# Filler products behind the last chunks of an edge pass, and one bank of sums fewer

## The chip, the cores and the metric

The kernel runs on one core of one Trainium2 chip. The metric is the device time of one execution in microseconds (us); lower is better. TensorE is the matrix engine, VectorE, ScalarE and GpSimd are the other three compute engines, SyncE issues transfers.

## What is computed

A graph network of four layers over 3125 nodes of 128 features and 50000 edges, sorted by target node. Each layer normalises the node features, passes them along the edges, sums at the targets and adds the result to the features. The change is in the third layer of the four (the reference's `_L2_gnn_ref`, "layer 2" in the kernel), which has two edge passes. The first one computes, cut to what matters:

```python
def _gat_layer(x, src, dst, W, a_src, a_dst, concat):      # 8 heads
    for h in range(W.shape[0]):
        Wh = x @ W[h]
        e = leaky_relu((Wh @ a_src[h])[src] + (Wh @ a_dst[h])[dst], 0.2)
        att = _seg_softmax(e, dst, n)
        out = segment_sum(att[:, None] * Wh[src], dst, num_segments=n)
...
def _rel_gcn_layer(x, src, dst, w, W):
    deg = segment_sum(w, dst, num_segments=n)
    norm = w / maximum(deg[dst], 1e-16)
    return relu(segment_sum(norm[:, None] * (x @ W)[src], dst, num_segments=n))
...
for i in range(2):
    x1 = _gat_layer(x1, src, dst, *gat_params[i], concat=i != 1)
    x2 = _rel_gcn_layer(x2, src, dst, edge_weight, gcn_params[i])
```

## The kernel before

The edges are cut into NC = 392 chunks of 128, and 8 chunks (BC) make a batch, so 49 batches (NBATCH). An edge pass of layer 2 is the stage `layer2_edges(i, ...)`, with i = 0 for the first and i = 1 for the second. Between the two stands a stage on the nodes (`layer2_nodes0`), behind the second one more and then the diffusion layer. The first pass begins when the tables of the node features lie in memory.

In a pass GpSimd gathers the 128 source rows of each chunk by an indirect transfer (recorded at L229) into a ring of RING = 40 chunks; a chunk's slot is free when TensorE has summed the chunk that stood in it. For each batch VectorE, ScalarE and TensorE work out the attention weights by turns: the windows are transposed on TensorE (L1704) and copied by ScalarE (L1800), the target's part of the logits is looked up (L1711), the logits are formed on VectorE (L1580, needs the gathered rows of the batch), transposed (L1717), scanned for their maxima, neighbouring batches exchange the maxima at their border (L1727 to L1732), and the exponentials are transposed back (L1739).

Then each chunk is summed on TensorE (`sums`). In the first pass VectorE has scaled the gathered rows by the weights (L1626), and TensorE multiplies them with a one-hot matrix of 17 columns: L1753 for the attention part, L1754 for the other, both float32, and L1759 in bf16 for the sums of the weights, which also tells the rest that the chunk is done. In the second pass the scaling is in the one-hot matrix, so that L1756 has 136 columns and L1757 has 17, and L1759 is the same. A float32 product stands in the trace as two records.

The sums of three chunks (PER = 3) stand in one bank of PSUM; with five banks (NBK, bank_of, L1481) the first chunk of a group may begin when ScalarE has stored the last chunk of the group five before. ScalarE stores a chunk (`store`, L1844 and L1847) seven chunks behind TensorE's order, and joins neighbouring groups by keeping the shared column (L1832, L1833), which VectorE adds (L1649, L1650).

The order is written out by hand and is the same on all engines: steps p (one for each batch, and four more) with ten slots q. A slot of TensorE's list may hold the sums of one chunk, then a transpose, look-up or exchange. A batch is looked up in step p = b and its chunks are summed a little over three steps later, so in step 48, the last one with a look-up, TensorE has 34 chunks left.

`busy(...)` (L1691) is a product that nothing reads: identity times a constant piece of memory, written to bank 7 (L1695). Before the change it works in the second pass alone: 24 of 512 columns ahead of the pass, three in each of the first slots, and behind each chunk one of 512, in the first steps also one of 256:

```python
sums(c)
busy(512, *(() if i and p >= min(nodes.begins) else (256,)))
```

Of the kernel before, what the change touches and what calls it, by code (L numbers as in the profile page):

```python
# [19 lines left out]
NC = 392  # L20
WIN = 16
H = 8
BC = 8
# [108 lines left out]
def build(nc, a, out):  # L132
    ctx = ExitStack()
    with ctx:
# [3 lines left out]
        banks = ctx.enter_context(nc.psum_tensor("banks", [P, 8, 512], F32))  # L138
# [39 lines left out]
        identb = keep.get([P], BF16)  # L178
# [1258 lines left out]
        SLOTS, AFTER, LEAD, PER = 10, 11, 2, 3  # L1437

        def layer2_edges(i, begin, nodes):
# [6 lines left out]
            RING = RB * BC  # L1446
# [31 lines left out]
            NGR = -(-NC // PER)  # L1478
            last_of = lambda g: min(PER * g + PER, NC) - 1

            NBK = 4 if i else 5  # L1481
            bank_of = lambda c: (4, 5, 6, 1, 7)[c // PER % NBK]
            sums_in = lambda c: banks[:, bank_of(c), 0:PS].rearrange("p (h w) -> p h w", w=HS)[:, :, c % PER * WIN:c % PER * WIN + WIN + 1]
            weights_in = lambda c: banks[0:3 * (H + 1), bank_of(c), PS + c % PER * WIN:PS + c % PER * WIN + WIN + 1]
            nb0, nc0, ng0, sh0 = i * NBATCH, i * NC, i * NGR, i * (NGR - 1)
# [19 lines left out]
            def g_landed(e, b):  # L1505
                e.wait_ge(of_rows[b % RB], rows0[b % RB] + 16 * BC * (b // RB + 1))
# [177 lines left out]
            def pe(e):  # L1684
                begin(e)
                if i:

                    e.wait_ge(t_made, 1)
                spare = wide.bitcast(BF16)[:, 0:512]

                def busy(*columns):  # L1691

                    if i:
                        for n in columns:
                            e.matmul(banks[:, 7, 0:n], identb, spare[:, 0:n], start=True, stop=True, skip_group_check=True)  # L1695

                busy(*[512] * 24)

                def turn(b):
                    e.wait_ge(e2_windows, nb0 + b + 1)  # L1700
                    if b:
                        e.wait_ge(e2_ot, nb0 + b)
                        e.wait_ge(e2_sum, nb0 + b)
                    e.transpose(banks[:, 0, :].bitcast(BF16)[:, 0:P], OHW[b % 2], identb).then_inc(e2_turned, 1)  # L1704

                def look_up(b):
                    e.wait_ge(e2_ot, nb0 + b + 1)
                    e.wait_ge(e2_bd, nb0 + b + 1)
                    if b:
                        e.wait_ge(e2_sum, nb0 + b)  # L1710
                    e.matmul(banks[:, 0, P:P + BC * H], OT[b % 2], BD[b % 2].rearrange("p j h -> p (j h)"), start=True, stop=True).then_inc(e2_edm, 1)  # L1711

                def turn_logits(b):
                    e.wait_ge(e2_z, nb0 + b + 1)
                    if b:
                        e.wait_ge(e2_ztc, nb0 + b)
                    e.transpose(banks[0:64, 2, 0:P], Z[b % 2], ident).then_inc(e2_zt, 1)  # L1717

                def exchange(b):
                    me = ML[b % R4]  # L1720
                    pr = ML[(b - 1) % R4] if b else None
                    ne = ML[(b + 1) % R4] if b < NBATCH - 1 else None
                    o = banks[0:64, 3, 0:2]
                    e.wait_ge(e2_bw, nb0 + min(b + 2, NBATCH))
                    if b:
                        e.wait_ge(e2_m2, nb0 + b)
                    e.matmul(o[:, 0:1], wide[0:64, P - H:P - H + 64], me[:, P - 1:P], start=True, stop=pr is None)  # L1727
                    if pr is not None:
                        e.matmul(o[:, 0:1], wide[0:64, P + 64 - H:P + 128 - H], pr[:, P - 1:P], start=False, stop=True)
                    x = e.matmul(o[:, 1:2], wide[0:64, P + H:P + H + 64], me[:, 0:1], start=True, stop=ne is None)  # L1730
                    if ne is not None:
                        x = e.matmul(o[:, 1:2], wide[0:64, P - 64 + H:P + H], ne[:, 0:1], start=False, stop=True)  # L1732
                    x.then_inc(e2_ex, 1)

                def turn_back(b):
                    e.wait_ge(e2_exp, nb0 + b + 1)
                    if b:
                        e.wait_ge(e2_a, nb0 + b)
                    e.transpose(banks[:, 3, P:P + 64], DF[b % 2], ident[0:64, 0:64]).then_inc(e2_back, 1)  # L1739

                def sums(c):
                    b, j = divmod(c, BC)
                    k4, k3, g = b % R4, b % R3, c // PER
                    begins = c % PER == 0
                    pv = sums_in(c)
                    rows = G[:, c % RING, :]
                    e.wait_ge(e2_spread, nc0 + c + 1)
                    g_landed(e, b)
                    if begins and g >= NBK:
                        e.wait_ge(e2_sacc, nc0 + PER * (g - NBK + 1))  # L1750
                    if i == 0:
                        e.wait_ge(e2_hi, b + 1)
                        e.matmul(pv[:, 0, :], rows[:, 0:D], OHF[k3][:, j, :], start=begins, stop=True, skip_group_check=True)  # L1753
                        e.matmul(pv[:, 1, :], rows[:, D + H:], OHV[k3][:, j, :], start=False, stop=True, skip_group_check=True)  # L1754
                    else:
                        e.matmul(pv[:, 0:H, :], rows[:, 0:D], S[c % RS][:, 0:H, :], start=begins, stop=True, skip_group_check=True)  # L1756
                        e.matmul(pv[:, H, :], rows[:, D + H:], S[c % RS][:, H, :], start=False, stop=True, skip_group_check=True)  # L1757
                    e.wait_ge(e2_split, nb0 + b + 1)
                    e.matmul(weights_in(c), AP[k3][:, j, :, :].rearrange("p k h -> p (k h)"), OH[b % RO][:, j, :],  # L1759
                             start=False, stop=True, skip_group_check=True).then_inc(e2_mm, 1)  # L1760

                for p in range(NBATCH + 4):
                    for q in range(SLOTS):
                        c = sums_at.get(SLOTS * p + q)
                        if SLOTS * p + q < 4 * SLOTS + AFTER + LEAD:
                            busy(512, 512, 512)
                        if c is not None:
                            sums(c)
                            busy(512, *(() if i and p >= min(nodes.begins) else (256,)))
                        if i:  # L1770
                            nodes.pe_at(e, p, q)
                        if q == 1 and p < NBATCH:
                            turn(p)
                        if q == 3 and 2 <= p < NBATCH + 2:
                            exchange(p - 2)
                        if q == 4 and p < NBATCH:
                            look_up(p)
                        if q == 8 and 2 <= p < NBATCH + 2:
                            turn_back(p - 2)
                        if q == 8 and p < NBATCH:  # L1780
                            turn_logits(p)

            def act(e):
# [92 lines left out]
                first.free()  # L1876

            return Stage(sp=sp, act=act, pool=pool, dve=dve, pe=pe)

        def l2_edges0_done(e):  # L1880
# [1538 lines left out]
        def regular_stages():  # L3419
            early = Early()  # L3420
            sums = layer1_sums(l0_edges_done, early)
            n1 = layer1_tables(l1_sums_done, early)
            m0, scored = layer2_mid(l2_edges0_done)
            wt = weights_t(scored, 4, n1.done, (STEPS - 1,))
            ends = EndNodes()
            m1 = layer2_end(ends)
            return [layer0_edges(early), sums, n1, Stage(sp=wt.sp), layer2_edges(0, n1.done, None), m0, Stage(act=wt.act, dve=wt.dve, pe=wt.pe),
                    layer2_edges(1, m0.done, ends), m1, diffusion(m1.done, ends)]
# [103 lines left out]
```

## Time and profile before

| | us |
|---|---|
| three runs, median | 2609.55 |
| three runs, lowest and highest | 2600.57 and 2618.6 |
| the profiled execution | 2596.79 |
| its span, from the first to the last instruction | 2595.0 |
| first edge pass of layer 2, first to last sum on TensorE | 767.4 to 1283.5 |
| second edge pass, from GpSimd's first gather to TensorE's last sum | 1323.6 to about 1900 |

The profile is of one execution. Times count from its first instruction. A busy TensorE means that products follow each other without a gap, not that it runs at its peak: ends are modelled. "PEclk" is the share of the full clock that TensorE was granted, 0.50 for the level of 1.2 GHz and 1.00 for that of 2.4 GHz; a mean between them is a stretch that had both. "PE" are products, "PEld" the weight loads, which may run beside them.

### The profile page before, as it was taken

How to read it: one execution, taken by the hardware profiler on the slowest of the kernel's cores; microseconds unless marked ns; L12 is line 12 of the kernel's file. 1: busy time of each engine (PE TensorE's matmuls, PEld its weight loads, DVE VectorE, ACT ScalarE, POOL GpSimd, SP SyncE). 2: the span in 40 equal slices, each digit the busy share in tenths (PEclk: the TensorE clock that was granted, in tenths of full speed). 3: DMA queues.
4: the chain of work that ended last, by engine and by line, in shares of the span. 5: the costliest groups of instructions: out<-in, count | busy, mean ns of one | idle time of the engine just before them, and what ended most of it. 6: DMA issues, size and time to landing. Idle time of an engine off the chain costs nothing.

```text
span 2595.0 us, 51123 instructions
## 1 busy us (share of the span) xinstructions
PE 2269.5 (87%) x12354; PEld 1940.0 (75%) x12453; DVE 1449.7 (56%) x6184; ACT 1228.3 (47%) x5343; POOL 1197.3 (46%) x1243
## 2 busy tenths in 40 slices
PE   3777777787539999999979999999989999999998
PEld 2555556554429999999947888888879889988887
DVE  5656556579535666666446676767643433334443
ACT  3667667675313333333234465645554444344443
POOL 3777777710057777777147777777330000000000
PEclk9966566589755555555589897979889999999999
DMA  3242442440334444444054444444452100000002
GB/s 91 61 126 64 126 126 64 126 114 5 93 101 106 111 109 110 109 108 134 20 133 107 110 115 113 114 105 114 153 218 77 29 18 16 18 26 26 26 25 62
DMA packets 174354, 227.42 MB, mean 88 GB/s; under 512 B 63551, under 2 KB 134408, under 8 KB 173928
## 3 DMA queue, kind: packets, MB, share of 16 engines
q0 software_dynamic: 50176, 131.74, 19.1%
q1 hardware_dynamic: 117070, 88.93, 11.3%
q10 hardware_dynamic: 6810, 3.40, 0.5%
q8 instruction: 111, 1.82, 0.3%
q14 instruction: 187, 1.53, 0.2%
HBM read 183.63 MB, written 40.29 MB: 86 GB/s over the span
## 4 chain that ended last, share of the span: by engine, by line
PE 71%; issue 9%; DVE 5%; ACT 4%; POOL 4%; DMA 4%; ACTq 2%; DVEq 0%; SPq 0%; POOLq 0%
PE banks L2790 9%; PE banks L2786 9%; PE banks L1753 7%; PE banks L1754 6%; PE banks L1695 5%; PE banks L1756 4%; POOL arena L229 4%; PE banks L1759 3%; PE banks L2792 3%; PE banks L733 3%; PE banks L2397 2%; PE banks L945 2%; PE banks L1757 2%; DMA arena<-h_table,arena 2%; PE banks L736 2%
## 5 line engine op out<-in xcount | busy, mean ns | idle before, releaser
L229 POOL DMA_INDIRECT arena<-value_table,arena x392 | 390.1, 995 | 318.6 <-DMA ed_table<-arena 199.4
L229 POOL DMA_INDIRECT arena<-gat_table,arena x392 | 403.1, 1028 | 200.4 <-issue 86.8
L2786 PE MATMUL banks<-counts,u_parts 128*128 128x448 f32 x1323 | 491.6, 372 | 3.1 <-DVE u_parts L2919 3.1
L2790 PE MATMUL banks<-counts_even,u_parts 128*128 128x448 f32 x1323 | 486.8, 368 | 0.0
L229 POOL DMA_INDIRECT arena<-h_table,arena x392 | 374.3, 955 | 119.5 <-issue 87.2
L2970 DVE CAST counts_even<-counts 128x448 fp32r<-128x448 bf16 x450 | 163.1, 390 | 304.0 <-PE banks L2790 279.6
L733 PE MATMUL banks<-arena 128*128 128x425 bf16 x392 | 196.0, 500 | 102.8 <-ACT arena L789 86.9
L2786 PEld LDWEIGHTS banks<-counts,u_parts 128*128 128x128 f32 x1323 | 249.6, 189 | 24.2 <-ACT arena L2414 3.3
L2790 PEld LDWEIGHTS banks<-counts_even,u_parts 128*128 128x128 f32 x1323 | 249.7, 189 | 21.5 <-ACT counts_even L2894 0.3
L736 PEld LDWEIGHTS banks<-arena 128*128 128x128 f32 x784 | 209.2, 289 | 69.7 <-issue 61.7
L1754 PE MATMUL banks<-arena 128*128 128x17 f32 x784 | 230.6, 375 | 0.0
L1753 PE MATMUL banks<-arena 128*128 128x17 f32 x784 | 228.2, 372 | 0.0
L786 ACT ACTIVATE arena<-banks 128x400 f32 x392 | 207.9, 530 | 36.3 <-DVE banks L722 25.7
L1844 ACT ACTIVATE arena<-banks 128x32 f32 (+1 forms) x784 | 187.3, 239 | 60.6 <-issue 38.6
L2894 ACT ACTIVATE counts_even<-counts 128x896 fp32r<-128x896 bf16 x123 | 117.4, 954 | 207.6 <-PE banks L2790 194.8
L1754 PEld LDWEIGHTS banks<-arena 128*128 128x128 f32 x784 | 214.2, 333 | 0.0
L1753 PEld LDWEIGHTS banks<-arena 128*128 128x128 f32 x784 | 201.9, 318 | 6.9 <-DVE arena L1626 0.2
L736 PE MATMUL banks<-arena 128*128 128x17 f32 x784 | 170.6, 298 | 30.2 <-DMA arena<-h_table,arena 29.4
L1695 PE MATMUL banks<-arena 128*128 128x512 bf16 (+1 forms) x540 | 189.2, 408 | 6.1 <-DMA ed_table<-arena 5.0
L1756 PE MATMUL banks<-arena 128*128 128x136 f32 x784 | 184.0, 320 | 2.3 <-issue 1.8
L1832 ACT ACTIVATE arena<-banks 128x2 f32<-128x2 f32 (+1 forms) x262 | 45.8, 175 | 287.6 <-PE banks L1759 228.9
L722 DVE TENSOR_TENSOR banks<-banks,arena 128x26 f32<-128x26 f32 x391 | 75.4, 193 | 181.6 <-ACT arena L778 176.7
(295 smaller groups left out, 4770.9 us busy)
## 6 DMA issues: line engine op xcount, KB each, us to landing
adj_rows<-arena SPq DMA_DIRECT2D x5, 4000.0 KB
arena<-ed_table SPq DMA_DIRECT2D x784, 0.5 KB
arena<-turned_rows SPq DMA_DIRECT2D x27, 448.0 KB, 3.3
counts<-adj_rows SPq DMA_DIRECT2D x1, 7200.0 KB, 20.3
arena<-h_table,arena POOLq DMA_INDIRECT x392
arena<-value_table,arena POOLq DMA_INDIRECT x392
arena<-gat_table,arena POOLq DMA_INDIRECT x392
counts<-adj_rows SPq DMA_DIRECT2D x1, 5600.0 KB, 17.5
```

Source lines behind the costliest of these rows:

```text
L229: return e.indirect_dma_start(into, None, table, bass.IndirectOffsetOnAxis(ap=index.bitcast(U32), axis=0))
L733: e.matmul(banks[:, c % RBANK, W1:CS], BY_LO[:, kx, :], BY_HI_D[:, kx, 0:CC], start=True, stop=True, skip_group_check=True)
L736: e.matmul(banks[:, c % RBANK, 0:W1], G[:, k, :], S[:, c // BC % 2, c % BC, :], start=False, stop=True, skip_group_check=True).then_inc(l0 ...
L786: e.activation(first.of(C, j), windows_in(j)[:, 1:, 0:WIN], ACT.Copy, scale=SMALL).then_inc(l0_counted, 1)
L1695: e.matmul(banks[:, 7, 0:n], identb, spare[:, 0:n], start=True, stop=True, skip_group_check=True)
L1753: e.matmul(pv[:, 0, :], rows[:, 0:D], OHF[k3][:, j, :], start=begins, stop=True, skip_group_check=True)
L1754: e.matmul(pv[:, 1, :], rows[:, D + H:], OHV[k3][:, j, :], start=False, stop=True, skip_group_check=True)
L1756: e.matmul(pv[:, 0:H, :], rows[:, 0:D], S[c % RS][:, 0:H, :], start=begins, stop=True, skip_group_check=True)
L1844: e.activation(first.of(acc, c), sums_in(c)[:, :, 0:WIN], ACT.Copy).then_inc(e2_acc, 1)
L2786: e.matmul(banks[:, 2 * r, 0:HALFW], weight, C_odd[:, w0:w0 + HALFW], start=start, stop=stop)
L2790: x = e.matmul(banks[:, 2 * r + 1, 0:HALFW], weight, tile(n), start=start, stop=stop)
L2970: e.tensor_copy(into, counts).then_inc(d_even_dve, 1)
```

## The change

The first pass gets filler products too, behind each chunk from WARM on. WARM is NC - RING - 2 * BC = 336 in the first pass, so that it is the last 56 chunks, and 0 in the second, where nothing changes. In the first pass the condition in the second line of the call is false, so that it gives a product of 512 columns and one of 256. They write to bank 7, which was the fifth bank of sums of the first pass; so this pass has four banks like the second, and the first chunk of a group waits for the stores of the group four before. The warm-up of 24 products and the fillers of the first slots stay with the second pass: the condition `if i` moves from inside `busy` to those two calls.

```diff
-            NBK = 4 if i else 5
-            bank_of = lambda c: (4, 5, 6, 1, 7)[c // PER % NBK]
+            NBK = 4
+            WARM = 0 if i else NC - RING - 2 * BC
+            bank_of = lambda c: (4, 5, 6, 1)[c // PER % NBK]
...
                 def busy(*columns):
 
-                    if i:
-                        for n in columns:
-                            e.matmul(banks[:, 7, 0:n], identb, spare[:, 0:n], start=True, stop=True, skip_group_check=True)
-
-                busy(*[512] * 24)
+                    for n in columns:
+                        e.matmul(banks[:, 7, 0:n], identb, spare[:, 0:n], start=True, stop=True, skip_group_check=True)
+
+                if i:
+                    busy(*[512] * 24)
...
-                        if SLOTS * p + q < 4 * SLOTS + AFTER + LEAD:
+                        if i and SLOTS * p + q < 4 * SLOTS + AFTER + LEAD:
                             busy(512, 512, 512)
                         if c is not None:
                             sums(c)
-                            busy(512, *(() if i and p >= min(nodes.begins) else (256,)))
+                            if c >= WARM:
+                                busy(512, *(() if i and p >= min(nodes.begins) else (256,)))
```

In TensorE's list before, around chunk 336, the first of the last 56 (L1753, L1754 and L1759 are a chunk, L1704 a transpose, L1727 to L1732 an exchange, L1711 a look-up, L1739 and L1717 transposes):

```order
L1704 MATMUL banks<-arena 128x128
L1753 MATMUL banks<-arena 128x17
L1754 MATMUL banks<-arena 128x17
L1759 MATMUL banks<-arena 27x17
L1727 MATMUL banks<-arena 64x1
L1729 MATMUL banks<-arena 64x1
L1730 MATMUL banks<-arena 64x1
L1732 MATMUL banks<-arena 64x1
L1753 MATMUL banks<-arena 128x17
L1754 MATMUL banks<-arena 128x17
L1759 MATMUL banks<-arena 27x17
L1711 MATMUL banks<-arena 128x64
```

And in the changed kernel, where from here on every line number of the stage is one higher (L1705 is L1704 of before) and L1695 is the filler:

```order
L1705 MATMUL banks<-arena 128x128
L1754 MATMUL banks<-arena 128x17
L1755 MATMUL banks<-arena 128x17
L1760 MATMUL banks<-arena 27x17
L1695 MATMUL banks<-arena 128x512
L1695 MATMUL banks<-arena 128x256
L1728 MATMUL banks<-arena 64x1
L1730 MATMUL banks<-arena 64x1
L1731 MATMUL banks<-arena 64x1
L1733 MATMUL banks<-arena 64x1
L1754 MATMUL banks<-arena 128x17
L1755 MATMUL banks<-arena 128x17
```

Two products come in behind the last one of the chunk, ahead of whatever followed it, here the exchange. Nothing else changes its place.

The end of TensorE's list for the pass, before (L1893 is the first product of the next stage, the sums of the weights):

```order
L1753 MATMUL banks<-arena 128x17
L1754 MATMUL banks<-arena 128x17
L1759 MATMUL banks<-arena 27x17
L1753 MATMUL banks<-arena 128x17
L1754 MATMUL banks<-arena 128x17
L1759 MATMUL banks<-arena 27x17
L1893 MATMUL banks<-arena 128x9 x25
```

And in the changed kernel:

```order
L1754 MATMUL banks<-arena 128x17
L1755 MATMUL banks<-arena 128x17
L1760 MATMUL banks<-arena 27x17
L1695 MATMUL banks<-arena 128x512
L1695 MATMUL banks<-arena 128x256
L1754 MATMUL banks<-arena 128x17
L1755 MATMUL banks<-arena 128x17
L1760 MATMUL banks<-arena 27x17
L1695 MATMUL banks<-arena 128x512
L1695 MATMUL banks<-arena 128x256
L1895 MATMUL banks<-arena 128x9 x25
```

The last pair stands between the last sum and the next stage. TensorE's whole list has 112 more products, 56 pairs.

## Rows read from the trace of the kernel before

**Rows 1.** The page: TensorE's granted clock in tenths, in 40 slices of the span.
```profile
PEclk9966566589755555555589897979889999999999
```

**Rows 2.** Stretches: busy us (records) of PE, PEld, DVE, ACT, POOL; clock; DMA share; GB/s.
```profile
900.00:1000.00 100.00, 100.00 (x505) 93.81 (x505) 61.74 (x320) 35.72 (x264) 76.84 (x77) 0.50 0.42 109
...
1213.00:1283.00 70.00, 70.00 (x347) 65.68 (x347) 34.84 (x184) 24.66 (x188) 22.38 (x24) 0.50 0.25 71
1283.00:1302.00 19.00, 16.59 (x77) 15.83 (x77) 9.80 (x12) 5.17 (x24) 0.00 (x0) 0.51 0.04 12
...
1360.00:1400.00 40.00, 39.15 (x275) 28.68 (x280) 21.14 (x101) 11.53 (x74) 30.56 (x32) 1.00 0.43 110
...
1558.00:1594.00 36.00, 34.86 (x161) 31.03 (x163) 19.08 (x95) 13.18 (x75) 27.82 (x27) 0.50 0.39 103
```

**Rows 3.** The first of TensorE's three waits in the first pass: us, times, longest.
```profile
PE banks L1717 <- DVE arena L1582: 2.5, 3, 1.5
```

**Rows 4.** GpSimd's last gather of the pass; from the chain, one landing at its start.
```profile
1241.44 0.95 POOL L229 DMA_INDIRECT arena<-value_table,arena  x1 [0.30 <-issue]
...
762.31 2.82 DMA arena<-value_table,arena
```

**Rows 5.** TensorE's timeline in the first pass: start, us, what.
```profile
1253.87 0.61 PE L1753 MATMUL banks<-arena 128*128 128x17 f32 x2
...
1254.96 0.61 PE L1753 MATMUL banks<-arena 128*128 128x17 f32 x2
...
1251.20 0.20 PE L1759 MATMUL banks<-arena 128*27 128x17 bf16 x1
1251.33 0.37 PE L1739 MATMUL banks<-arena 64*128 64x64 f32 x1
```

**Rows 6.** TensorE's timeline in the second pass at the low clock, with fillers (L1695).
```profile
1568.79 0.61 PE L1695 MATMUL banks<-arena 128*128 128x512 bf16 x1
1569.19 0.66 PE L1756 MATMUL banks<-arena 128*128 128x136 f32 x2
...
1570.15 0.61 PE L1695 MATMUL banks<-arena 128*128 128x512 bf16 x1
...
1571.51 0.61 PE L1695 MATMUL banks<-arena 128*128 128x512 bf16 x1
1572.05 0.37 PE L1739 MATMUL banks<-arena 64*128 64x64 f32 x1
```

**Rows 7.** Groups of TensorE's products from 1213 to 1284 us, by shape.
```profile
L1711 PE MATMUL banks<-arena 128*128 128x64 f32 x8 | 2.8, 449 | 0.0
L1727 PE MATMUL banks<-arena 64*64 64x1 f32 x12 | 2.2, 253 | 0.0
L1739 PE MATMUL banks<-arena 64*128 64x64 f32 x6 | 2.2, 367 | 0.0
...
L1704 PE MATMUL banks<-arena 128*128 128x128 bf16 x4 | 1.2, 288 | 0.0
```

**Rows 8.** Timeline: the first product of the stage behind the pass.
```profile
1285.43 10.83 PE L1893 MATMUL banks<-arena 27*128 27x9 f32 x50 [1.91 <-ACT arena L1847]
```

**Rows 9.** Timeline: the store of chunk 29 and the first product of chunk 39.
```profile
819.30 0.17 ACT L1847 ACTIVATE arena<-banks 27x16 f32 x1
...
820.78 0.40 PE L1753 MATMUL banks<-arena 128*128 128x17 f32 x1
```

**Rows 10.** TensorE's waits in the second pass: L1756 for ScalarE's stores.
```profile
PE banks L1756 <- ACT arena L1847: 0.2, 1, 0.2
```

**Rows 11.** Groups of TensorE's products from 1558 to 1594 us, by shape.
```profile
L1695 PE MATMUL banks<-arena 128*128 128x512 bf16 x16 | 9.7, 608 | 0.0
...
L1759 PE MATMUL banks<-arena 128*27 128x17 bf16 x18 | 3.5, 195 | 0.0
```

**Rows 12.** TensorE's timeline in the second pass at the high clock, both fillers.
```profile
1395.21 0.50 PE L1695 MATMUL banks<-arena 128*128 128x512 bf16 x2
...
1396.12 0.50 PE L1695 MATMUL banks<-arena 128*128 128x512 bf16 x2
```

## The prediction

> **What bounds the kernel now.** I read the picture in slices first, then the stretches, then the waits, then single products. The slices show TensorE's granted clock in tenths: from the 12th to the 20th it stands at 5, half of full speed [rows 1]. That is layer 2's first edge pass. The stretches give it in numbers: between 900 and 1000 us the matrix engine is busy 100.00 of 100 us at a granted clock of 0.50 (the 1.2 GHz level), VectorE 61.74, ScalarE 35.72, GpSimd 76.84 [rows 2]. The list of what TensorE waited for in the whole pass begins with 2.5 us for VectorE's logits [rows 3]; two smaller entries follow, and none names ScalarE's stores. So the pass is bound by TensorE at its low level, and what is put behind a chunk there is paid for unless it lies beside a weight load.
>
> GpSimd is close behind. Its last gather of the pass begins at 1241.44 us [rows 4]; TensorE's last stretch, from 1213 us, still has 70.00 of 70 us of work at 0.50 [rows 2]. In that stretch lie the 56 chunks that the change touches: the 336th starts at 1213.07 us and the last one ends at 1283.5.
>
> **The products themselves.** One chunk of the first pass is L1753, L1754 and L1759. From one L1753 to the next it is 1254.96 - 1253.87 = 1.09 us [rows 5]. Only 17 columns are streamed in each, so what takes the time is the four float32 weight loads. In the last stretch 56 chunks take 61 us, and the 9 us beside them are transposes and look-ups of the last batches.
>
> **The change, part by part.** 1. Two filler products (512 and 256 columns, bf16) go behind each of the last 56 chunks, 112 instructions. No wait is added, no DMA and no other engine's instruction. The trace of before does not show this filler in the first pass, but it shows it in the second, where it stood already, at both levels of the clock. The question is which of the two levels applies; I take the low one, for reasons given below. At the low level a chunk of the second pass with 512 columns takes 1570.15 - 1568.79 = 1.36 us, of which .40 lies between the filler and L1756 [rows 6]. Against the 1.09 of the first pass that is .27 us for 512 columns, less than the .43 us that they stream at 1.2 GHz, since the first weight load of the next chunk is done beside the filler. The further 256 columns have no load left to hide and cost 256/1.2 GHz = .21. That gives .48; the next product in the first pass streams 17 columns, not 136, so it may go down to .45. I take .46.
>
> Where the filler is followed by a float32 product of 64 rows, nothing is hidden: L1695 at 1571.51 to L1739 at 1572.05 is .54 [rows 6], where in the first pass L1739 stood .13 behind L1759 [rows 5]. So it costs .13 + .54 + .21 - .13 = .75. I take the same for L1727, which also has 64 rows. L1704 is a bf16 product of 128 rows with a short load; I take its full streaming time, 768/1.2 GHz = .64. L1711 is float32 with 128 rows, as L1753, and gets .46.
>
> How many of each: the groups of the last stretch show L1727 12 times (two records for a product, so 6), L1739 6, L1711 8 (4) and L1704 4, of which one begins before the first filler (3) [rows 7]. Fillers between chunks: 55, as the last one stands behind the last sum. That one costs nothing: TensorE is idle there for 1.91 us until ScalarE has stored the last sums [rows 8], and .64 us lies inside it. The rest of the 55, 36, is followed by the next chunk at once. The sum is (36 + 4) x .46 + 3 x .64 + 12 x .75 = 18.4 + 1.9 + 9.0 = 29.3 us.
>
> Bounds of this term from both sides: below, the 24.8 us of 55 x .45 while the clock stays low, and a gain if it does not (rival A); above, 55 x .75 = 41 us, if no load is ever hidden. Of the two I am nearer the lower one, as its row is the same pair filler and float32 product of 128 rows.
>
> The Trainium skill, "TensorE: Matmul & The Clock Gate", Part 3, "What overlaps and what doesn't", says that a weight load overlaps a product in flight only where the row groups differ. By that rule the first load of the next chunk would not hide behind the filler, and the sum would be the 41 us of the upper bound. The trace speaks against it here: L1756, 128 rows behind a filler of 128 rows, starts after .40 us, less than the filler streams.
>
> 2. Four banks of sums in place of five. No instruction is added; the wait of every third chunk for ScalarE's stores now asks for a group that is three chunks younger. Queued behind that wait on TensorE is the rest of the pass. I followed the 127 group starts against the end of the store that they would now wait for (L1847). The least room is at chunk 39: the store of chunk 29 ends at 819.30 + .17 = 819.47 us, the product starts at 820.78, so 1.31 us of room [rows 9]. The median is 3.65 us, and in the last stretch it is never under 2.79. The engine with room is ScalarE, 35.72 busy of 100. So this part costs 0, with 0 as the near end. The far end: the second pass runs with four banks at a mostly high clock and its waits of L1756 for L1847 come to 0.2 us in all [rows 10]; a gain is excluded, as waiting for a younger store is never sooner. Fillers make TensorE later and the room larger.
>
> 3. The first filler wait (t_made) and the warm-up of 24 products stay with the second pass alone, and the fillers between the slots too. Nothing of the second pass changes.
>
> **Why the clock stays low.** TensorE at 100 of 100 us busy held 0.50 for the whole pass; busy time alone does not bring the high level. It is 1.00 in the second pass, which begins with 24 fillers of 512 in a row [rows 2]. But in the second pass it also fell and stayed at 0.50 from 1558 to 1594 us [rows 2], with a filler of 512 behind nearly every chunk (16 for 18) [rows 11]. There a chunk's 1.36 us hold .43 us of filler and two records of 136 float32 columns, each of which goes through twice (.23 us a record at 1.2 GHz, so .45). A chunk of the last stretch, 1.09 + .46 = 1.55 us, would hold .64 us of filler, and its own products of 17 columns stand behind their loads. It streams for a smaller part of its time than those chunks did, and they stayed low for 36 us; nor is there a burst ahead of it. So I take the low level to the end of the pass.
>
> The Trainium skill, the same page, Part 1, "What's actually happening", says that the throttled clock is the default and that activity of the matrix engine releases it. Read by busy time, that rule would have the first pass at 2.4 GHz already; the trace does not agree (100.00 of 100 us at 0.50). Read by what is streamed it is the rule of rival A, which the change would then meet.
>
> **Sum.** The profiled execution has a span of 2594.96 us, printed as 2595.0, in a time of 2596.79; 29.3 more give 2626. The median of the three runs shown is 2609.55, 12.8 above the profiled one, and the runs spread over 18 us. On the median the forecast is 2609.55 + 29.3 = 2638.9 us, 1.1% more. A measurement tells about 1%, 26 us, from no change, so the forecast lies just beyond it.
>
> **The rivals.** A. The fillers bring 2.4 GHz (faster than before). Place: within the first chunks after 1213 us. For it: the second pass ran 1360 to 1400 us at 1.00 with this same pair of fillers, a chunk every 1396.12 - 1395.21 = .91 us [rows 12]. Against it: that pass came to it with a burst, and its low stretches above. Price: 56 chunks at .91 would be 51 us in place of 61. But the last gather begins at 1241.44 and a landing takes about 4 us from there (.94 of issue, .30 and 2.82 as at the start of the pass, [rows 4]), so the last batch can't be looked at before 1245.5; 34 of the chunks stand behind it in the order. From there 34 x .91 + some 3 us for what lies between end at about 1279.5, 4 us sooner. If the high level lasts into the node stage (16.59 busy at 0.51 [rows 2]), up to 8 more. So 4 to 12 us: about 2602. The case decides itself by one thing, the granted clock in the last stretch.
>
> B. No load is hidden: 41 us, 2651. For it the .54 before L1739, against it the .40 before L1756.
>
> C. The fourth bank comes too late: ScalarE's stores slip by over 1.31 us behind TensorE's third chunk. Then the early groups, where the room is 1.31 to 1.58 us three times, wait. At 1 us for each of the first dozen batches this is 10 us at most beside the fillers: 2649. ScalarE's idle time speaks against it.
>
> D. The change does not do what it says: the fillers would be hidden where TensorE has idle time in the tail. The trace has 70.00 busy of 70, so only the last one is.
>
> **How the numbers follow.** Forecast 0.76, A 0.09, B 0.11, C and D 0.04 together. The likeliest's own range is 2630 to 2648: 24.8 to 31 us and some 6 us of the runs' own spread. The range that should hold 8 in 10 is 2618 to 2653. Over 1% slower means beyond 2635.6: from the forecast about six parts in ten (0.46), from B and C 0.14, together 0.60. Within 1%: 0.30 from the forecast and 0.07 from A, 0.37. Faster by over 1%: 0.03, A with the clock's luck in later stages.
>
> **What would show it.** A granted clock of 0.50 between the first filler (near 1213 us) and the end of the pass; chunks with the pair of fillers 1.55 us apart; a stretch of about 99 us in place of 70; L1739 .75 further behind L1759; no entry of ScalarE's L1847 in TensorE's waits; the second pass as long as before, only later. A clock of 1.00 there, or chunks .9 us apart, makes the forecast wrong; a distance of 1.85 us between chunks makes B right; waits for L1847 make C right.

## The result and the profile after

The changed kernel took 2636.9 us (median of 10 runs, 2623.25 to 2661.75), the kernel before 2608.69 us (median of 10, 2598.47 to 2624.36). The ratio is 1.0116 with a 95% interval from 1.0086 to 1.0146: slower by 22 to 38 us. Forecast were 2638.9 us and 29.3 us more than before.

The granted clock in 40 slices, as in [rows 1]:

```profile
PEclk9856666688655555555589969798589999999999
```

The fives of the first edge pass reach from the 12th to the 20th slice, as they did before. The stretches follow, with columns as in [rows 2]. Chunk 336 starts at 1220.2 us here, 7.1 us later than before. The row by itself is of the kernel before, from its chunk 336 on:

```profile
900.00:1000.00 100.00, 99.55 (x502) 92.91 (x502) 59.75 (x315) 36.23 (x264) 76.89 (x76) 0.50 0.41 107
1220.20:1319.60 99.40, 99.40 (x459) 75.52 (x458) 34.80 (x184) 25.86 (x195) 25.14 (x26) 0.50 0.19 53
1319.60:1336.00 16.40, 15.37 (x71) 14.26 (x70) 8.25 (x9) 2.74 (x14) 0.00 (x0) 0.50 0.00 0
...
1848.00:1930.00 82.00, 81.98 (x368) 69.82 (x367) 39.65 (x193) 32.26 (x177) 29.04 (x29) 0.50 0.39 129
```

```profile
1213.00:1283.40 70.40, 70.40 (x349) 66.04 (x348) 34.84 (x184) 24.97 (x190) 22.38 (x24) 0.50 0.25 71
```

The second row answers to the row of before. It is 99.4 us long against 70.4 (99.4 against 70.3 from the start of chunk 336's first product to that of the last sum), TensorE is busy in all of it, and the clock is 0.50 throughout. The 110 records more are the 55 pairs up to the last sum. The span of this execution, 2659.9 us, is 65 us over that of before; only 29 lie here. The pass began 3.3 us later and took 3.8 more ahead of chunk 336, and the second edge pass took 584 us from its first gather to its last sum, against 556: the row from 1848 us shows 82 us of it at the low clock. That profile was the longest of the ten runs, and the median does not carry that excess; a run below asks whether it belongs to the change.

TensorE's timeline, for [rows 5] and [rows 6] (a chunk is now L1754, L1755 and L1760, and L1740 was L1739):

```profile
1226.02 0.82 PE L1695 MATMUL banks<-arena 128*128 128x512 bf16 x2
1226.64 0.45 PE L1754 MATMUL banks<-arena 128*128 128x17 f32 x2
...
1227.57 0.82 PE L1695 MATMUL banks<-arena 128*128 128x512 bf16 x2
...
1229.12 0.82 PE L1695 MATMUL banks<-arena 128*128 128x512 bf16 x2
1229.87 0.37 PE L1740 MATMUL banks<-arena 64*128 64x64 f32 x1
```

From filler to filler it is 1.55 us, as worked out. L1754 stands .62 behind the pair, less than the .64 that 768 columns take to stream at 1.2 GHz, so its weights were loaded beside the filler. L1740 with its 64 rows stands .75 behind it (.54 + .21 in the sum). At the end of the pass the last pair lies beside ScalarE's stores, as said, and leaves .53 us of the 1.91 idle in [rows 8]:

```profile
1319.70 0.82 PE L1695 MATMUL banks<-arena 128*128 128x512 bf16 x2
1321.06 2.30 PE L1895 MATMUL banks<-arena 27*128 27x9 f32 x10 [0.53 <-ACT arena L1849]
```

What TensorE waited for in the whole pass, for [rows 3]: still the logits, and no store. (The stores, L1844 and L1847 before, are L1846 and L1849 here, two lines further down and not one.)

```profile
PE banks L1718 <- DVE arena L1583: 8.4, 7, 5.7
PE banks L1705 <- ACT arena L1796: 1.2, 1, 1.2
PE banks L1760 <- DVE arena L1644: 0.5, 1, 0.5
...
769.10 0.42 PE L1718 MATMUL banks<-arena 128*64 128x128 f32 x1 [5.71 <-DVE arena L1583]
```

The 8.4 us against the 2.5 of [rows 3] are no change: 5.71 of them are the wait for the pass's first logits. The kernel before has it too, 5.73 us, but it ends at 765.75 us there, ahead of the pass as it was counted, and here it falls into the count.

### The profile page after: what moved, and what is told of

It is laid out like the page before. It is cut to its first block, busy times and chain, and to the rows that moved or that the text cites. A ratio compares the mean times of both kernels' runs of the same rounds, so it can differ in the third digit from the quotient of the medians.

```text
span 2659.9 us, 51447 instructions
## 1 busy us (share of the span) xinstructions
PE 2362.5 (89%) x12565; PEld 1978.7 (74%) x12565; DVE 1446.9 (54%) x6184; ACT 1230.1 (46%) x5343; POOL 1205.1 (45%) x1243
## 4 chain that ended last, share of the span: by engine, by line
PE 71%; issue 9%; DVE 5%; POOL 5%; ACT 4%; DMA 4%; ACTq 1%; DVEq 0%; SPq 0%; POOLq 0%
PE banks L2792 9%; PE banks L2788 9%; PE banks L1695 7%; PE banks L1754 6%; PE banks L1755 6%; POOL arena L229 4%; PE banks L1757 4%; PE banks L1760 3%; PE banks L2794 3%; PE banks L733 3%; PE banks L2399 2%; PE banks L945 2%; PE banks L1758 2%; PE banks L736 2%; DMA arena<-h_table,arena 2%
## 5 line engine op out<-in xcount | busy, mean ns | idle before, releaser
L229 POOL DMA_INDIRECT arena<-value_table,arena x392 | 397.2, 1013 | 321.7 <-DMA ed_table<-arena 202.6
L1695 PE MATMUL banks<-arena 128*128 128x512 bf16 (+1 forms) x717 | 267.3, 435 | 4.6 <-DMA ed_table<-arena 4.6
L1755 PE MATMUL banks<-arena 128*128 128x17 f32 x784 | 230.6, 375 | 0.0
L1754 PE MATMUL banks<-arena 128*128 128x17 f32 x784 | 224.7, 368 | 0.0
L1846 ACT ACTIVATE arena<-banks 128x32 f32 (+1 forms) x784 | 187.9, 240 | 61.2 <-issue 39.1
L1754 PEld LDWEIGHTS banks<-arena 128*128 128x128 f32 x784 | 202.5, 319 | 17.0 <-issue 6.9
L1755 PEld LDWEIGHTS banks<-arena 128*128 128x128 f32 x784 | 214.2, 333 | 0.0
L1757 PE MATMUL banks<-arena 128*128 128x136 f32 x784 | 193.0, 333 | 0.1
L722 DVE TENSOR_TENSOR banks<-banks,arena 128x26 f32<-128x26 f32 x391 | 75.5, 193 | 181.7 <-ACT arena L778 177.0
```

What stands on the lines that cost most here:

```text
L229: return e.indirect_dma_start(into, None, table, bass.IndirectOffsetOnAxis(ap=index.bitcast(U32), axis=0))
L1846: e.activation(first.of(acc, c), sums_in(c)[:, :, 0:WIN], ACT.Copy).then_inc(e2_acc, 1)
```

## The experiments

Four questions were put: is the cost the fillers' or the bank's, what decides the cost of one filler, can the clock be lifted, and what would it be worth. The runs came onto two kinds of chip. On the one the kernel before takes 2605 us (2608.69 in the comparison above); on the other 2959 to 2981. What makes the second kind slower was not followed up; in the first edge pass TensorE idles there for some 75 us (below). Ratios are always against the kernel before on the same chip. "The stretch" is the time from the first product of chunk 336 to the last sum of the pass, 70.3 us in the profile before; a burst ahead of chunk 336 is not in it. Each figure of a stretch is from the one execution that was profiled.

**1. The bank alone (e1_banks).** Four banks and no filler in the first pass; on the slower chip.

```diff
-                            if c >= WARM:
+                            if i:
```

> Four banks of sums in the first pass and no filler there. My theory (the banks cost nothing, the room in front of each group is 1.3 us or more): the stretch from chunk 336 to the last sum stays at 70.4 us, no wait of TensorE for the stores, and the time is that of before within 6 us. Rival (the fourth bank comes too late): waits for L1847 of the stores appear and the pass is up to 10 us longer.

Ratio 0.9998, from 0.997 to 1.0026. TensorE's waits in the pass, the three longest of ten entries, and the longest that names ScalarE:

```profile
PE banks L1754 <- issue: 41.1, 25, 4.0
PE banks L1754 <- DVE arena L1627: 17.7, 6, 6.4
PE banks L1705 <- issue: 12.5, 7, 2.5
...
PE banks L1740 <- ACT arena L1812: 1.4, 1, 1.4
```

No entry names a store. The stretch was 75.5 us and not 70.4, so that part of the expectation missed; but TensorE was busy in it for as long as before, and what is more is idle time of this chip:

```profile
1431.00:1506.60 75.60, 70.62 (x349) 66.07 (x348) 34.71 (x185) 25.04 (x190) 21.95 (x22) 0.50 0.22 63
```

So the fourth bank costs nothing that this comparison can tell: its interval leaves room for 8 us either way. On the faster chip the evidence is the list of waits of the changed kernel above. This row is the one without fillers for the other runs on slower chips.

**2. One filler, two sizes (e2_512 and e4_256).** On the same slower chip; only 512 columns, or only 256, behind each of the 56 chunks.

```diff
-                                busy(512, *(() if i and p >= min(nodes.begins) else (256,)))
+                                busy(512, *((256,) if i and p < min(nodes.begins) else ()))
```

```diff
-                            if c >= WARM:
-                                busy(512, *(() if i and p >= min(nodes.begins) else (256,)))
+                            if i:
+                                busy(512, *(() if p >= min(nodes.begins) else (256,)))
+                            elif c >= WARM:
+                                busy(256)
```

> Only the product of 512 columns behind each of the last 56 chunks. Theory (clock at 0.50, one weight load of .17 us hides beside the filler where the next product is float32 with 128 rows): a plain chunk takes 1.34 us (1.55 less .21), the stretch is 40 x .25 + 3 x .43 + 12 x .54 = 17.8 us longer than the 70.4 of before, so 88. Rival (no load is hidden): 55 x .54 = 30 us longer, 100 us.

> Only a product of 256 columns behind each of the last 56 chunks. Theory of the hidden load: a plain chunk takes 1.12 us against 1.09 without a filler, and the stretch is 40 x .03 + 3 x .21 + 12 x .33 = 5.8 us longer, 76 us, and the kernel within 1% of before. Rival (a filler costs its streaming and its own start): 55 x .33 = 18 us longer, 88 us.

With 512: ratio 1.0058 (1.0026 to 1.009), the stretch 90.8 us. With 256: ratio 1.0000 (0.997 to 1.0031), the stretch 81.4 us. The stretches, e2_512 first:

```profile
1423.60:1514.40 90.80, 88.32 (x403) 73.59 (x403) 34.65 (x184) 25.56 (x193) 21.30 (x22) 0.50 0.18 53
```

```profile
1424.20:1505.70 81.50, 76.98 (x403) 68.86 (x403) 34.56 (x184) 25.24 (x190) 21.37 (x22) 0.50 0.20 59
```

TensorE's busy time rose from 70.6 by 17.7 and by 6.4 us; forecast were 17.8 and 5.8, and the rival that hides no load said 30 and 18. The stretches themselves rose by 15.3 and 5.9, since on this chip a part of the fillers falls into idle time. A chunk with 256 columns, in the timeline of e4_256:

```profile
1470.29 0.39 PE L1695 MATMUL banks<-arena 128*128 128x256 bf16 x1
1470.48 0.45 PE L1754 MATMUL banks<-arena 128*128 128x17 f32 x2
1470.77 0.59 PE L1755 MATMUL banks<-arena 128*128 128x17 f32 x2
...
1471.41 0.40 PE L1695 MATMUL banks<-arena 128*128 128x256 bf16 x1
1471.74 0.37 PE L1740 MATMUL banks<-arena 64*128 64x64 f32 x1
```

1.12 us from filler to filler, where a chunk without one takes 1.09 [rows 5]: a product of 256 columns at the low clock costs .03 us there. Ahead of L1740 it costs .33. So about .18 us of a filler is free where a 128-row float32 product follows, and nothing ahead of the 64-row ones.

**3. Fillers left out where 64 rows follow (e7_skip).** On the faster chip, beside a trace of the kernel before on the same chip (e8_before). Of the 14 pairs left out, 12 stood ahead of a 64-row float32 product and 2 ahead of a chunk.

```diff
-                            if c >= WARM:
+                            if c >= WARM and (i or q not in (3, 8)):
```

> The kernel before once more, for a trace from the same chip as the other runs of this call. On the chip of the prediction the stretch from chunk 336 to the last sum was 70.3 us. On the chip of the first experiments the run without a filler had 75.5, with some us of TensorE's time idle. I expect the one or the other.

> The changed kernel without the 14 pairs of fillers that stand in the slots 3 and 8: 12 of them stand ahead of a float32 product of 64 rows (L1728, L1740), two ahead of a chunk. Theory (what a filler costs is decided by what follows it: .75 us ahead of 64 rows, .46 ahead of a chunk): 12 x .75 + 2 x .46 = 9.9 us less than the change costs, so the stretch is 19 us longer than that of before and not 29. Rival (all fillers cost the same, 29.1/55 = .53 us): 41 x .53 = 22 us longer.

The kernel before: 2604.65 us, the stretch 70.3 us again. Without the 14 pairs: ratio 1.0067 (1.0031 to 1.0103) and a stretch of 89.4 us, 19.1 longer than before, where 19 were forecast and 22 by the even price:

```profile
1217.30:1306.80 89.50, 87.17 (x424) 73.66 (x430) 34.83 (x184) 25.82 (x195) 24.67 (x26) 0.50 0.20 59
```

A quarter of the fillers made a third of the cost. The row's 87.17 us busy in 89.50 is no idle time. The stretch has 424 records where 431 are due (459 of the changed kernel less 28), and each of the seven gaps of .33 us stands where a filler of 512 columns has no record. The product behind such a gap comes no later than where both fillers are recorded.

**4. A burst ahead of the fillers (e3_burst, e5_hold, e12_hold2).** e3_burst, slower chip, is the changed kernel with 16 fillers of 512 ahead of chunk 336; e5_hold, faster chip, has two of 512 behind each chunk besides; e12_hold2, slower chip, has more of them beside the exchange. The first of these edits is in all three kernels, the second in e5_hold, the third in e12_hold2.

```diff
+                            if not i and c == WARM:
+                                busy(*[512] * 16)
                             sums(c)
```

```diff
-                                busy(512, *(() if i and p >= min(nodes.begins) else (256,)))
+                                busy(512, *((512,) if not i else () if p >= min(nodes.begins) else (256,)))
```

```diff
+                            elif c >= WARM and p < NBATCH - 1:
+                                busy(*[512] * {3: 4, 4: 3}.get(q, 2))
+                            elif c >= WARM:
+                                busy(512, 256, *((512,) if q in (3, 4) else ()))
```

> As the changed kernel, with 16 fillers of 512 in a row ahead of chunk 336. It gives what the change had not: a burst. Theory (the fillers failed since nothing lifted the clock first, as rival A of the prediction says a high clock would be worth 4 to 12 us before the burst is paid): the granted clock is 1.00 behind the burst, chunks stand 0.9 us apart, 5 to 7 us are paid for the burst, then TensorE waits some us for the last gathers. If the clock outlives that wait, the stretch is about 67 us; if it falls there, the last 34 chunks take 1.55 us each again and the stretch is about 90 us. Rival (the clock can't be lifted in this stretch): clock 0.50 throughout and 99.5 + 6.8 = 106 us.

> 16 fillers of 512 ahead of chunk 336, then two of 512 behind each of the 56 chunks. In the run with the burst and the change's own fillers the clock rose and fell again after 10 us. Theory (the high clock is worth next to nothing here even if it is held, since the last gathers end the pass): the clock stays at 1.00 from the burst to the last sum or nearly so, a chunk takes 1.0 us, and the stretch from chunk 336 on takes 60 to 66 us, which with the 6 us of the burst is what it took before, 70; the time is within 1% of before. Rival (the high clock is worth 10 us and more): the stretch takes under 58 us. If the clock falls again, the stretch is over 90 us.

> The burst ahead of chunk 336 as before, and behind the 56 chunks two fillers of 512, four in slot 3 (ahead of an exchange), three in slot 4; from the last look-up on 512 and 256, and one more of 512 in the slots 3 and 4. The run with two of 512 and no more lost the high clock in a stretch that held an exchange. Theory (the clock falls where TensorE streams least, at the exchange, and more fillers beside it keep it up): 1.00 from the burst to the end of the pass, chunks .9 to 1.0 us apart, and on the faster chip the stretch from chunk 336 takes 60 to 64 us (70.3 before), with the burst 66 to 70: no more than 5 us gained in the pass. So rival A of the prediction was not worth its chance even where the clock is held. Rival (something other than the exchange ends the high level): it falls again within 15 us, and the stretch is over 95 us.

| | ratio (interval) | clock 1.00 for | stretch |
|---|---|---|---|
| e3_burst, slower chip | 1.0073 (1.0036 to 1.0111) | 9 us and a little | 94.1 |
| e5_hold, faster chip | 1.0148 (1.0105 to 1.019) | 13 us | 101.3 |
| e12_hold2, slower chip | 1.0086 (1.0056 to 1.0116) | 20 us | 99.1 |

The stretches of e3_burst:

```profile
1428.00:1435.00 7.00, 7.00 (x24) 3.83 (x24) 2.63 (x14) 1.94 (x16) 5.48 (x6) 0.50 0.33 85
1436.00:1445.00 9.00, 8.91 (x70) 6.79 (x68) 3.98 (x23) 1.92 (x15) 5.48 (x6) 1.00 0.32 89
1445.00:1530.00 85.00, 84.38 (x388) 64.08 (x388) 30.09 (x160) 22.61 (x172) 11.63 (x12) 0.50 0.14 39
```

The burst does lift the clock: the rival by which it can't be lifted here falls. It fell again each time, sooner than each of the three expectations had it. In e3_burst it fell near 1445.7 us and the last gather began only at 1461.3, so that reason of mine for a fall was wrong. A wait of .64 us stands in front of that fall:

```profile
1444.42 0.50 PE L1695 MATMUL banks<-arena 128*128 128x512 bf16 x2
1445.56 0.29 PE L1705 MATMUL banks<-arena 128*128 128x128 bf16 x1 [0.64 <-ACT arena L1829]
```

Where it fell in e5_hold, 1235.2 us, the 3 us before were an exchange and what stands beside it, and no wait:

```profile
1232.34 0.60 PE L1695 MATMUL banks<-arena 128*128 128x512 bf16 x2
1232.87 0.27 PE L1728 MATMUL banks<-arena 64*64 64x1 f32 x2
...
1233.43 0.40 PE L1754 MATMUL banks<-arena 128*128 128x17 f32 x2
...
1234.32 0.38 PE L1695 MATMUL banks<-arena 128*128 128x512 bf16 x1 [0.16 <-issue]
```

(The .16 us in the last line are again a missing record: one of this chunk's two fillers is not in the trace.) In e12_hold2 the clock outlived the exchange at 1454.7 us, with four fillers ahead of it, and fell at 1462, after a wait of 1.02 us and an L1740:

```profile
1459.95 0.40 PE L1754 MATMUL banks<-arena 128*128 128x17 f32 x2 [1.02 <-issue]
...
1461.15 0.27 PE L1740 MATMUL banks<-arena 64*128 64x64 f32 x1
```

This fall came after 20 us, so the rival's 15 us missed too, though its stretch of over 95 us came. So the high level ended once behind an exchange with no wait, and twice behind a wait, of .64 and 1.02 us. That is the order in time. Which of the two, the thin products or the wait, ends it was not separated. In none of the three did it last to the end of the pass; what the stretch would take at the high clock was not measured. The rate was: in e3_burst it is .90 us from one pair of fillers to the next, as in [rows 12].

```profile
1440.39 0.50 PE L1695 MATMUL banks<-arena 128*128 128x512 bf16 x2
...
1441.29 0.50 PE L1695 MATMUL banks<-arena 128*128 128x512 bf16 x2
```

**5. Fillers in the whole pass (e6_whole, e9_spread, e11_spread).** e6_whole has 24 of 512 ahead, three in each of the first slots, and 512, 512 and 256 behind each chunk, on the faster chip. The other two are one kernel, with 16 more ahead of chunk 0, and the fillers spread as in e12_hold2.

```diff
-                if i:
-                    busy(*[512] * 24)
+                busy(*[512] * 24)
...
-                        if i and SLOTS * p + q < 4 * SLOTS + AFTER + LEAD:
+                        if SLOTS * p + q < 4 * SLOTS + AFTER + LEAD:
...
-                            if c >= WARM:
-                                busy(512, *(() if i and p >= min(nodes.begins) else (256,)))
+                            busy(512, *((512, 256) if not i else () if p >= min(nodes.begins) else (256,)))
```

> Fillers in the whole first pass, as in the second: 24 of 512 ahead, three in each of the first slots, and 512, 512 and 256 behind each chunk. Theory (the first pass could run at the high clock from its first product on, and is then bound by the gathers, 1.25 to 1.3 us each): granted clock 1.00 in most of the pass, the last sum 8 to 12 us sooner than before on the first chip, and the kernel 0.2 to 0.8% faster. Rival (the clock falls in some wait and cannot rise again by these fillers, since at the low level a chunk then takes 1.09 + .28 + .43 + .21, about 2.0 us): from there on TensorE is .7 us slower for each chunk, and the kernel is 20 to 250 us slower.

> Fillers in the whole first pass again, spread so that there is more of them beside the exchange, where TensorE streams least and where the clock fell in the runs before: 24 of 512 ahead, three in the first slots, 16 ahead of chunk 0; behind a chunk two of 512, four in slot 3 and three in slot 4; from the last look-up on 512 and 256, and one more of 512 in the slots 3 and 4. Theory (the high clock falls at the exchanges, and once held it makes the pass bound by the gathers and the last 34 chunks take .9 us): 1.00 through the pass in all runs or nearly all, the last sum at 1262 to 1275 us against 1284, the kernel 10 to 25 us faster than before. Rival (no amount of spreading makes it safe): a part of the runs is over 2700 us again, as with the run before.

> The same kernel as the last one with fillers in the whole first pass. On the slower chip all six of its runs lost the high clock, in the profile after TensorE had waited 7.9 us for ScalarE 64 us into the pass, and took 270 us more. On the faster chip, where TensorE hardly waits in this pass, the theory has it hold: last sum at 1262 to 1275 us, 10 to 25 us faster than before. Rival (it falls there as well): some runs over 2700 us.

e6_whole took 2605.39, 2621.98, 2809.06 and 2928.59 us in its four runs, before 2605.45 (median of 15). The profile is of the run of 2621.98, in which the clock held for the whole pass:

```profile
900.00:1000.00 100.00, 97.78 (x725) 73.25 (x738) 61.84 (x322) 36.96 (x273) 75.59 (x77) 1.00 0.42 110
1244.00:1290.00 46.00, 45.15 (x329) 33.66 (x333) 20.33 (x111) 16.01 (x123) 0.00 (x0) 1.00 0.02 5
```

And it was not faster, as far as two runs can tell. A chunk with its three fillers at the full clock takes 1.11 us, and one without a filler at the low clock takes 1.09 [rows 5]:

```profile
1288.03 0.71 PE L1695 MATMUL banks<-arena 128*128 128x512 bf16 x3
...
1289.14 0.71 PE L1695 MATMUL banks<-arena 128*128 128x512 bf16 x3
```

GpSimd does 77 gathers in 100 us as it did in [rows 2], the last gather starts at 1242.8 us (1244.9 in e8_before), and the last sum is at 1290.1 against 1284.3. What the clock gave, the fillers that keep it took. (TensorE was busy in all of the pass, and the 97.78 are short by missing records: there are 725 of products to 738 of weight loads, and the gaps in the pass, 70 in all, are of .16 us ahead of a group of fillers that lacks one.) The part of the expectation with 8 to 12 us of gain missed. The other part, 20 to 250 us more, was met by one of the other two runs and exceeded by the second: 200 and 320 us are paid. Neither has a profile; their mean granted clocks, 0.813 and 0.774, are below the 0.886 and 0.894 of the two shorter ones, which fits a level that was lost on the way, but does not show it.

The spread kernel ran on the slower chips only, six and four runs: 3225 to 3241 us and 3247 to 3266, ratios 1.0921 (1.0887 to 1.0956) and 1.093 (1.0881 to 1.0978). Both expectations of a held clock missed. Both profiles lost the level 68 us after it had been taken, and did not have it again in this pass; e9_spread:

```profile
908.00:976.00 68.00, 67.63 (x418) 42.62 (x416) 29.47 (x150) 15.61 (x97) 28.02 (x28) 1.00 0.22 58
977.00:1770.00 793.00, 792.56 (x3214) 550.70 (x3213) 278.94 (x1461) 173.22 (x1276) 310.47 (x324) 0.50 0.23 60
```

In the expectation of e11_spread I put that down to a wait of 7.9 us. That was misread: this wait stands ahead of the stretch of 1.00. What stands in front of the fall at 976.0 us is a wait of .37 us and an L1739; in e11_spread it is a wait of .85 us at the same place of the order:

```profile
973.12 0.40 PE L1753 MATMUL banks<-arena 128*128 128x17 f32 x2 [0.37 <-issue]
...
974.32 0.27 PE L1739 MATMUL banks<-arena 64*128 64x64 f32 x1
```

These two waits, like that of 1.02 us in e12_hold2, end within .1 us of the end of VectorE's scaling of the chunk's rows (L1627), though the profile says "issue": VectorE was late there. At the low level a chunk of the spread kernel with two fillers of 512 takes 1.76 us (the median in e9_spread) against 1.09 without one, which is most of the 270 us that one loss costs. Whether the spread kernel would hold on the faster chip stays open. No version was found that beats the kernel before.

**6. The changed kernel again (e10_after),** on a slower chip.

> The changed kernel once more. Its first profile had a span of 2659.9 us, 65 over that of before, of which only 29 lie in the stretch of the fillers; in the second edge pass its clock was at 0.50 for one stretch of 82 us. Theory (the change costs its 29 us in the stretch and nothing after it; the rest was the clock of the second pass, which differs from run to run): the stretch takes 99.4 us again, the kernel is 1.1% slower than before, and the profiled second pass is between 560 and 600 us from its first gather to its last sum (before 556 and 564, the first profile of the changed kernel 584). Rival (a later start of the second pass makes its clock worse): the second pass is over 580 us again.

Ratio 1.0069 (1.003 to 1.0108). TensorE's busy time in the stretch is 99.76 us, 29.1 more than the 70.62 of e1_banks, while the stretch is 25.5 longer, since 3.7 us of the fillers fall into idle time:

```profile
1427.30:1528.30 101.00, 99.76 (x458) 75.31 (x457) 34.55 (x184) 25.88 (x195) 21.46 (x22) 0.50 0.16 47
```

The second pass took 687.8 us from its first gather to its last sum, against 706.4 in e1_banks and 697.0 in e2_512 on such chips, so the 560 to 600 us of the expectation did not fit this chip, but the rival falls: a second pass that starts later is not longer for it. On the faster chip e5_hold settles it as well: its second pass starts at 1363.4 us, later than the 1360.2 of the changed kernel, and takes 562 us, against 556 and 564 in the two profiles of the kernel before. The 28 us of the first profile of the changed kernel were that one execution's.

## Why the prediction was right

The forecast was 29.3 us in the stretch and 1.1% in all; measured were 29.1 us in the stretch and 1.16% (0.86 to 1.46).

- **The bound.** TensorE at 0.50, busy throughout, was the bound of the last 56 chunks. Every microsecond of filler that no load hid came out at the end: 29.1 us more busy time on both kinds of chip, 29.1 more of stretch on the one without idle time, 25.5 on the other. In the medians it was 28.2 us; that these come within 2 us of the forecast is in part luck, since the interval alone is 16 us wide.
- **The clock.** It stayed at 0.50, as forecast from a stretch of the second pass that had stayed low with more to stream. The fillers could not lift it; a burst of 16 could (e3_burst). So rival A needed something the change did not have. Its price of 4 to 12 us was never reached either: where the clock held for the whole pass, in e6_whole, the last sum came 6 us later than before. That run had heavier fillers than the rival, so the price itself is not refuted, only that such fillers earn it.
- **The size.** .46 for a chunk (measured 1.55 less 1.09), .75 ahead of 64 rows (measured .75 behind the pair and .13 ahead of it, less the .13 of before). The product L1705 was put at .64 and cost .61. The two sizes of filler landed within 1 us of the same arithmetic in busy time, which the rival without hidden loads misses by 12 us; the run with 14 pairs left out did so in its stretch, where the even price misses by 3. Against the rule of the Trainium skill named in the prediction ("TensorE: Matmul & The Clock Gate", Part 3, "What overlaps and what doesn't") the trace stands as before: 128 rows behind 128 rows did overlap, .03 us for 256 columns in e4_256. Ahead of a float32 product of 64 rows nothing was hidden. Why these differ no run here shows.
- **The banks.** Nothing that could be told from none, as said: 0.9998 (0.997 to 1.0026), and no store among the waits.
- **What was off.** The prediction gave the high clock a chance through the fillers alone and did not say what ends it. In the five profiles in which a burst or fillers had brought it in the first pass and it was lost again there, it ended once behind an exchange and four times behind a wait of .37 to 1.02 us. The second pass "as long as before" did not show in the first profile (584 us against 556); the runs above put that down to the execution.

## What to carry to other kernels

A filler product is not free because nobody reads it. Behind an engine that is itself the bound it cost here its streaming time, less the weight load that it hid, and it can pay only if the clock rises. Whether it will can be judged, as here, from stretches of the same trace that had the same products at the low level and stayed there. Count what stands behind each filler before placing it, and do not build on a clock that a single wait may take away: in the spread kernel one such loss cost about 270 us, and where the clock was held for a whole pass it gave nothing.

## What was not expected

- A product of 256 columns behind a chunk at the low clock costs .03 us ahead of a 128-row float32 product and .33 us ahead of a 64-row one.
- The granted clock held for the 519 us of the pass in e6_whole, through every exchange, with three fillers behind each chunk and no wait of TensorE, and was lost elsewhere behind a wait as short as .37 us. In the same kernel two runs of four were 200 and 320 us longer.
- Small gaps in a busy TensorE, of .16 us at the high clock and .33 at the low one, were products without a record. The weight loads of the same product, which are in the trace, tell such a gap from a wait.
- The same program takes 2605 to 2609 us on two chips and 2959 to 2981 on three others. In the first pass of e1_banks TensorE is idle for 75.8 us (591.6 less 515.8 busy), mostly under "issue", that is for nothing the profile names, where its waits came to 4 us before. VectorE waits there too: in 100 us of that pass 39.8 us in L1609, the first step behind the exchange of the maxima, for something the profile calls "remote", where the same step (L1608) waited 16.6 us for TensorE's exchange before. The cause stays open. The rows, e1_banks first:

```profile
DVE arena L1609 <- remote: 39.8, 8, 6.3
...
DVE arena L1608 <- PE banks L1732: 16.6, 10, 1.8
```
